# Decoder kernel: expert units in pairs, 512 columns per elementwise operation, new order tables

## What is computed

```python
probs = jax.nn.softmax(logits)
top_vals, top_idx = jax.lax.top_k(probs, K)             # K = 4, renormalised
comb = zeros((N, E)).at[arange(N)[:, None], top_idx].add(top_vals)
g = jnp.einsum('nh,ehi->eni', h, w_gate)                # E = 16, i = 176
u = jnp.einsum('nh,ehi->eni', h, w_up)
y = jnp.einsum('eni,eih->enh', silu(g) * u, w_down)
routed = jnp.einsum('enh,ne->nh', y, comb)
shared = silu(h @ sh_gate) * (h @ sh_up) @ sh_down      # 704 wide
out = routed + sigmoid(h @ sh_gate_w) * shared
```

## Time and profile before

| | us |
|---|---|
| median of 3 runs (lowest, highest) | 955.67 (949.19, 959.2) |
| the profiled execution, its whole time | 949.86 |
| its span from first to last instruction | 947.7 |
| PE busy | 828.1 (87%) |
| DVE busy | 631.5 (67%) |
| ACT, POOL busy | 369.4 (39%), 358.1 (38%) |

### The profile page before, as it was taken

One profiled execution on the slowest core, in us unless ns is written; L12 is line 12 of the kernel. 1 busy time (PEld: TensorE's weight loads), 2 busy tenths in 40 slices (PEclk: granted clock), 3 DMA queues, 4 the chain that ended last, 5 costly groups with the idle time before them and its releaser, 6 DMA issues.

```text
span 947.7 us, 12835 instructions
## 1 busy us (share of the span) xinstructions
PE 828.1 (87%) x4575; PEld 629.4 (66%) x4600; DVE 631.5 (67%) x1322; ACT 369.4 (39%) x796; POOL 358.1 (38%) x390
## 2 busy tenths in 40 slices
PE   6897656989999898889999997889999898679997
PEld 5675445753788786753788786753788786426886
DVE  5242699785456999884456999895456999764333
ACT  5121555327325444326324444327324444253110
POOL 4302396121034875220034976121034976000322
PEclk9998757999999999998999999999999999999999
DMA  7202400011026340311016340311024340300442
GB/s 224 102 12 82 154 36 0 1 56 60 1 63 226 118 131 0 112 67 50 1 55 232 117 129 6 111 48 68 1 57 150 117 134 0 111 2 1 145 155 78
DMA packets 26930, 76.13 MB, mean 80 GB/s; under 512 B 3436, under 2 KB 5420, under 8 KB 26228
## 3 DMA queue, kind: packets, MB, share of 16 engines
q1 hardware_dynamic: 26612, 75.26, 24.2%
q10 hardware_dynamic: 256, 0.07, 0.0%
HBM read 74.13 MB, written 1.11 MB: 79 GB/s over the span
## 4 chain that ended last, share of the span: by engine, by line
PE 53%; DVE 24%; issue 10%; POOL 7%; ACT 4%; DMA 1%; ACTq 0%; DVEq 0%; POOLq 0%; SPq 0%
PE B L806 26%; PE F L806 19%; DVE arena L1477 7%; POOL arena L493 3%; PE B L1107 3%; DVE arena L1489 3%; DVE nmx L1549 2%; PE F L835 1%; DVE q_t L1610 1%; ACT big L773 1%; DVE arena L1310 1%; POOL arena L567 1%; PE F L817 1%; DVE q_t L1615 1%; POOL rs L473 1%
## 5 line engine op out<-in xcount | busy, mean ns | idle before, releaser
L806 PE MATMUL B<-spare,mw 128*128 128x256 f32 x880 | 210.5, 383 | 6.3 <-DVE q_t L1615 5.1
L806 PEld LDWEIGHTS B<-spare,mw 128*128 128x128 f32 x880 | 164.6, 191 | 31.7 <-issue 8.5
L1477 DVE TENSOR_TENSOR_SCAN arena<-F,arena 128x512 f32<-128x512 f32 x128 | 148.8, 1206 | 1.6 <-ACT F L733 1.5
L584 POOL TENSOR_TENSOR spare<-q_t 128x256 f32<-128x256 f32 x112 | 80.7, 729 | 173.2 <-DVE q_t L1615 160.4
L493 POOL TENSOR_TENSOR arena<-du,arena 128x1024 f32<-128x1024 f32 x60 | 140.9, 2363 | 12.9 <-PE B L888 12.9
L733 ACT ACTIVATE F<-delta,a_neg 128x255 f32<-128x255 f32 x256 | 109.7, 467 | 58.2 <-DVE arena L1477 58.2
L806 PE MATMUL B<-mw,spare 128*128 128x256 f32 x448 | 117.6, 388 | 0.0
L795 ACT ACTIVATE q_t<-B 128x256 f32<-128x256 f32 x112 | 41.9, 380 | 149.9 <-PE B L806 149.8
L806 PEld LDWEIGHTS B<-mw,spare 128*128 128x128 f32 x448 | 86.5, 195 | 14.1 <-issue 1.6
L773 ACT ACTIVATE big<-B 128x512 f32<-128x512 f32 x128 | 69.4, 594 | 51.1 <-PE B L806 38.5
L1610 DVE SCALAR_TENSOR_TENSOR q_t<-q_t,B 128x256 f32<-128x256 f32 x112 | 46.6, 416 | 57.3 <-ACT q_t L795 57.0
(11 more groups left out here) (246 smaller groups left out, 1323.8 us busy)
## 6 DMA issues: line engine op xcount, KB each, us to landing
mw<-in_w_moe SPq DMA_DIRECT2D x112, 384.0 KB, 3.1
room<-in_w_f SPq DMA_DIRECT2D x4, 2544.0 KB, 9.2
arena<-b_out SPq DMA_DIRECT2D x32, 256.0 KB, 5.3
room<-in_w_l SPq DMA_DIRECT2D x4, 768.0 KB, 6.9
w_m<-in_w_m SPq DMA_DIRECT2D x1, 2112.0 KB
room<-in_w_l SPq DMA_DIRECT2D x4, 512.0 KB, 5.0
x_t<-in_x_t SPq DMA_DIRECT2D x4, 256.0 KB, 3.7
x_tok<-in_x_tok SPq DMA_DIRECT2D x4, 256.0 KB, 6.6
```

The source lines that it names most:

```text
L584: g.tensor_tensor(hid1[0:r, m % HID_RING, :], hraw[0:r, m % 3, :], crs[0:r, int(m >= MTE), :], ALU.mult)\
L806: return t_.matmul(dst, lhsT, rhs, start=start, stop=stop, skip_group_check=True)
L1477: v.tensor_tensor_scan(h, F[i][:, :], h, 0.0, ALU.mult, ALU.add)\
```

## The change

Two units 2p and 2p + 1 form a pair. `be{2p}` is now the gate half of pair p: PE puts both gates (4 calls) into one bank, K[0]; ACT takes one tanh of 512 columns; DVE makes `(tanh + 1) * gate` with 512 columns (`st{p}`). `be{2p+1}` is the up half: both ups (4 calls) into K[1], then the downs of pair p - 1 (4 calls); DVE multiplies by up with 512 columns (`gu{p}`), POOL multiplies by the routing row with 512 columns (`hid{p}`). Everything stays in one ring of three pairs (`PAIR_RING`), in place. PE waits at a gate half for `st{p-1}` and at an up half for `gu{p-1}`; in the last batch odd pairs use F[0], F[1] and the lag is two pairs. ACT waits for `hid{p-3}`. SP loads two units at the odd phases. The last pair keeps two 256-column products on DVE. Matmuls and bytes are the same.

```diff
...
+        thg = ao[:, 2:8, :].rearrange("p (r u) t -> p r (u t)", u=2)
...
+        def pair_banks(b, p):
+            return F[0:2] if b == B - 1 and p % 2 else K[0:2]
+        def pair_lag(b):
+            return 2 if b == B - 1 else 1
+        def pair_ring(p):
+            return thg[:, p % PAIR_RING, :]
...
+                if ph in BE and BE.index(ph) % 2 and BE.index(ph) >= 3:
+                    p = BE.index(ph) // 2
+                    for m in (2 * p - 2, 2 * p - 1):
+                        if m + MW_RING < MT1:
+                            sp.wait_ge(*pb.at(f"down{m}", b))
+                            sp.dma_start(mw[:, m % MW_RING, :], ins["w_moe"][m + MW_RING])\
+                                .then_inc(mw_in[m % MW_RING], 16)
...
+                if ph in BE and BE.index(ph) % 2:
+                    p = BE.index(ph) // 2
...
+                    pool.wait_ge(*db.at(f"gu{p}", b))
+                    if p >= HID_RING // 2:
+                        pool.wait_ge(*pb.at(f"down{2 * p + 1 - HID_RING}", b))
+                    s = 2 * p % HID_RING
+                    g.tensor_tensor(hid1[:, s:s + 2, :], pair_ring(p).rearrange("p (u t) -> p u t", u=2),
+                                    crs[:, int(2 * p >= MTE), :].unsqueeze(1).to_broadcast([P, 2, S]), ALU.mult)\
+                        .then_inc(gb.step(f"hid{p}"), 1)
...
+                if ph in BE and BE.index(ph) % 2 == 0:
+                    p = BE.index(ph) // 2
+                    act.wait_ge(*pb.at(f"g{p}", b))
+                    if p >= PAIR_RING:
+                        act.wait_ge(*gb.at(f"hid{p - PAIR_RING}", b))
+                    a.activation(pair_ring(p), pair_banks(b, p)[0][:, :], ACT.Tanh, scale=0.5)\
+                        .then_inc(ab.step(f"th{p}"), 1)
...
+                    p, u = divmod(BE.index(ph), 2)
+                    lag = pair_lag(b)
+                    if p >= lag:
+                        pe.wait_ge(*db.at(f"gu{p - lag}" if u else f"st{p - lag}", b))
+                    for j in range(2 if 2 * p + 1 < MT1 - 1 or u == 0 else 1):
+                        m = 2 * p + j
+                        slot = m % MW_RING
+                        if u == 0:
+                            pe.wait_ge(mw_in[slot], b * (len(range(slot, MT1, MW_RING)) * 16) + (m // MW_RING) * 16 + 16)
                         for k in range(KT):
                             c = u * D + k * P
+                            last = mm(pair_banks(b, p)[u][:, j * S:j * S + S], mw[:, slot, c:c + P], x5t[:, k, :],
                                       k == 0, k == KT - 1)
+                    last.then_inc(pb.step(f"u{p}" if u else f"g{p}"), 1)
+                    if u and p >= 1:
+                        expert_down(b, 2 * p - 2)
+                        expert_down(b, 2 * p - 1)
...
+                    p, u = divmod(BE.index(ph), 2)
+                    gates, ups = pair_banks(b, p)
+                    th = pair_ring(p)
+                    if u == 0:
+                        dve.wait_ge(*ab.at(f"th{p}", b))
+                        v.scalar_tensor_tensor(th, th, 1.0, gates[:, :], ALU.add, ALU.mult)\
+                            .then_inc(db.step(f"st{p}"), 1)
+                    else:
+                        dve.wait_ge(*pb.at(f"u{p}", b))
+                        dve.wait_ge(*db.at(f"st{p}", b))
+                        if 2 * p + 1 < MT1 - 1:
+                            v.tensor_tensor(th, th, ups[:, :], ALU.mult).then_inc(db.step(f"gu{p}"), 1)
...
```

More of the change, by code:

```diff
@@ L46 @@
 HID_RING = 4
+PAIR_RING = 3
 HALF = P // 2
@@ L341, in head @@
             return 8 * (q // 2) + 2 * j + q % 2
-        def gate_bank(b, m):
-            return K[m % (3 if b == B - 1 else 2)]
+        def pair_banks(b, p):
[4 more added lines that the diff above has]
+            return thg[:, p % PAIR_RING, :]
         def y_bank(dp):
@@ L788, in back @@
                     copy(crs.rearrange("p m n -> p (m n)"), K[3][:, :], ab, "crs", scale=0.5)
-                if ph in BE:
-                    m = BE.index(ph)
-                    act.wait_ge(*pb.at(f"gu{m}", b))
-                    if m >= 3:
-                        act.wait_ge(*db.at(f"gu{m - 3}", b))
-                    r = P if m < MT1 - 1 else HALF
-                    a.activation(thg[0:r, m % 3, :], gate_bank(b, m)[0:r, 0:S], ACT.Tanh, scale=0.5)\
-                        .then_inc(ab.step(f"th{m}"), 1)
+                if ph in BE and BE.index(ph) % 2 == 0:
[5 more added lines that the diff above has]
+                        .then_inc(ab.step(f"th{p}"), 1)
             run(front, back, af, ab, ORDER)
@@ L1208, in back @@
                 if ph in BE:
-                    m = BE.index(ph)
-                    slot = m % MW_RING
-                    pe.wait_ge(mw_in[slot], b * (len(range(slot, MT1, MW_RING)) * 16) + (m // MW_RING) * 16 + 16)
-                    r = 3 if b == B - 1 else 2
-                    if m >= r:
-                        pe.wait_ge(*db.at(f"gu{m - r}", b))
-                    for u in range(2 if m < MT1 - 1 else 1):
+                    p, u = divmod(BE.index(ph), 2)
[7 more added lines that the diff above has]
+                            pe.wait_ge(mw_in[slot], b * (len(range(slot, MT1, MW_RING)) * 16) + (m // MW_RING) * 16 + 16)
                         for k in range(KT):
                             c = u * D + k * P
-                            last = mm(gate_bank(b, m)[:, u * S:u * S + S], mw[:, slot, c:c + P], x5t[:, k, :],
+                            last = mm(pair_banks(b, p)[u][:, j * S:j * S + S], mw[:, slot, c:c + P], x5t[:, k, :],
                                       k == 0, k == KT - 1)
-                    last.then_inc(pb.step(f"gu{m}"), 1)
-                    if m >= 3:
-                        expert_down(b, m - 3)
+                    last.then_inc(pb.step(f"u{p}" if u else f"g{p}"), 1)
+                    if u and p >= 1:
+                        expert_down(b, 2 * p - 2)
+                        expert_down(b, 2 * p - 1)
                 if ph == "bout":
-                    for m in range(MT1 - 3, MT1):
+                    for m in range(MT1 - 2, MT1):
                         expert_down(b, m)
@@ L1605, in back @@
                 if ph in BE:
-                    m = BE.index(ph)
-                    dve.wait_ge(*ab.at(f"th{m}", b))
-                    r = P if m < MT1 - 1 else HALF
-                    up = gate_bank(b, m)[:, S:2 * S] if m < MT1 - 1 else gate_bank(b, m)[HALF:P, 0:S]
-                    v.scalar_tensor_tensor(thg[0:r, m % 3, :], thg[0:r, m % 3, :], 1.0, gate_bank(b, m)[0:r, 0:S], ALU.add,
-                                           ALU.mult).then_inc(db.step(), 1)
-                    if m >= 3:
-                        dve.wait_ge(*gb.at(f"hid{m - 3}", b))
-                    own(db, b)
-                    v.tensor_tensor(hraw[0:r, m % 3, :], thg[0:r, m % 3, :], up, ALU.mult)\
-                        .then_inc(db.step(f"gu{m}"), 1)
+                    p, u = divmod(BE.index(ph), 2)
[10 more added lines that the diff above has]
+                            v.tensor_tensor(th, th, ups[:, :], ALU.mult).then_inc(db.step(f"gu{p}"), 1)
+                        else:
+                            v.tensor_tensor(th[:, 0:S], th[:, 0:S], ups[:, 0:S], ALU.mult).then_inc(db.step(), 1)
+                            v.tensor_tensor(th[0:HALF, S:2 * S], th[0:HALF, S:2 * S], gates[HALF:P, S:2 * S], ALU.mult)\
+                                .then_inc(db.step(f"gu{p}"), 1)
                 if ph == "bout":
```

35 lines of the change are left out of this document (10 added, 25 removed), and 12 rows, old and new, of tables (AFTER_DVE, AFTER_PE).

## The result

The changed kernel takes 949.40 us (median of 20 runs, 947.07 to 950.81), the kernel before, run beside it, 955.94 (20 runs, 949.19 to 959.31 and two far above, 1020.13 and 1383.35, which the ratio leaves out). The ratio is 0.9944, 95% interval [0.9927, 0.9961]: 0.56% less, where 944 against 955.67 (-1.2%) was forecast. The profiled executions are 949.86 us before (span 947.7) and 950.81 after (span 949.0). So the two traces do not show the 6.5 us between the medians (5.6 without those two runs): they differ by +1.3 us of span. Before's trace comes from one of its shortest executions, after's from its longest.

The account below looks back on a forecast made before the run. PE bounds the kernel overall, DVE sets the scan's pace with PE close behind. Three merged stretches x (-2.8 - 0.3 - 1.2) = -12.9, +1.6 gives -11.3: 938.6, plus 5.8 carried over, 944 us; range 932 to 958.

Parts of the forecast that it names:

- Scan stage: First scan to output product in each merged stretch: 71.3 us against 74.1, so -2.8 us.
- The two waits that were followed: DVE in the scan stage: about 0.9 us for pair 7's tanh after s2, 0.4 for the ups of pair 6.
- Into the scan: Stretch ahead of the first scan, pair 4's gates moved behind d1: scan starts about 0.3 us earlier.
- +0.6 if the tanh is late: Bound ahead of the first scan: a late be8 tanh removes the cover, then +0.6 us.
- Head pairs to `ob`: Head stage of each merged stretch: DVE's waits go as maxima run beside the projection, -1.2 us, bounds -2.4 and +1.
- Attention of the back: Front scores to fa1 and behind, one more item ahead and one less after: 0, between -1.5 and +1.5 us.
- Last batch: PE-bound experts of the last batch: +0.5 us at the start, +1.1 at the end, together +1.6.
- The sum's frame: Whole-kernel total: the median's 5.8 us above before's profiled execution carried over, turning 938.6 into 944.4 us.
- the saving is eaten: Rival, chance 0.30: pairs' waits push PE back, scan keeps 1 us of gain, head stage gives nothing: 953 us.
- The slower rival: Rival, chance 0.12: PE waits for pairs at its banks in merged stretches, +4.2 us per stretch: 970 us.
- The rule of the Trainium skill: Cited with the slower rival (0.12): small idles between matmul groups cycling PSUM banks make PE's clock swing; about 1.6 us per stretch.

Follow-up runs that it names:

- second trace: The kernel before, unchanged, run and profiled once more: 953.94 us, ratio 1.0006, profiled span 952.5.
- last experiment: The kernel before with 2 throwaway matmuls ahead of each of the scores bm14 and bm15 in the merged stretches: 950.77 us, ratio 0.9981.
- ninth experiment: The changed kernel with filler at at0, before's attention positions and be8 behind d2, its 512-column pair operations cut into two of 256: 946.95 us.
- third experiment: The changed kernel with before's positions up to fg3 on PE, DVE and ACT, the new ones behind: 949.40 us, ratio 0.9973.
- fifth experiment: The changed kernel with five throwaway matmuls in PE's 2.50 us gap at at0: 948.13 us, ratio 0.9939.
- sixth experiment: The changed kernel with new positions up to the maxima behind oa, before's from there up to fg3: 949.52 us, ratio 0.9969.
- Three edits: On the changed kernel: be8 behind d2 (949.33 us), filler matmuls at at0 (948.13), before's attention positions behind oa (949.52); all together 939.95, ratio 0.9866.
- its twin: The changed kernel with at0 filler, before's attention positions and be8 behind d2, without extra last-batch filler: 939.95 us; with that extra filler 942.62.

## Why the prediction was right or wrong

**Scan stage, right in place, too large in the saving.** 71.3 us were forecast and 71.29, 71.30, 71.31 measured. DVE's prices were 682 and 685 (684 taken), POOL's 1,270 (1,350 taken; of the two bounds the lower, 1,278, was the right one: the broadcast routing row costs nothing), ACT's 591. The two waits that were followed are there, 0.9 for a tanh and 0.4 for ups, in the waits of the changed kernel inside the stage (columns as above):

```profile
DVE q_t L1624 <- ACT q_t L805: 1.2, 2, 0.9
DVE q_t L1630 <- PE B L816: 0.4, 1, 0.4
```

What was wrong is the base: 74.1 was the second stretch, the only one of the three with a low-clock piece early in its scan. Before's busy table there:

```profile
531.50:535.00 3.50, 3.50 (x11) 2.84 (x10) 3.40 (x4) 1.74 (x4) 3.50 (x3) 0.51 0.00 0
```

The stages beside it are 73.49 and 73.26. The saving was 2.3 on average, -7.0 in the trace where -8.4 stood. At full clock the stage of before is 73.24 (second trace) to 73.50 (last experiment), so the saving is 1.9 to 2.2 us, of which 1.1 is the width (ninth experiment) and the rest the pairing with its positions. The prices held: 73.24 less 0.4 of waits is 72.8 us of DVE's work, 71.30 less 1.6 is 69.7, and the prediction had 72.8 and 69.8. What was mis-sized are the waits of before: the 1.3 us that were left over in the stretch with the piece are 0.4 at full clock, so the new 1.6 took 1.2 us off the saving and not 0.2.

**Into the scan, right.** -0.2 for -0.3. The bound "+0.6 if the tanh is late" was not reached, but `be8` stood in the path: one phase later gives another 0.78.

**Head pairs to `ob`, the step that failed first.** The waits of DVE that were to go did go. The prediction named `bq3` behind the first head pair as a cost of copies (+1 at most). It costs through PE instead: the transposes had filled a gap, the gap of 2.50 us stayed empty, and PE ran its next eight records in 2.90 instead of 1.55 us. 29.51 became 31.0, so -1.2 became 0 by the mark. And the term was wrong even at full clock: the variance comes 1.5 us earlier, but the back's first exponential does not (30.29 us behind the head masks, 30.19 in before), so the gain returns as a longer next stage. The waits view of before could have told: PE's idle time at that place was 0.52 only because 1.95 us of `bq3` stood in front of it.

**Attention of the back, the other side of the same step.** Taken as 0 within 1.5, measured from the variance to the sum at full clock 37.96 against 36.04 in the last experiment, and 36.25 in the third with a low-clock piece: +1.7 to +1.9 per stretch, outside the bounds. The prediction looked only at what stands between `ob` and `fa1` and took the start as given. PE in order of time, after:

```profile
424.47 1.97 PE L816 MATMUL F<-room,arena 128*128 128x256 f32 x8
426.28 0.59 PE L816 MATMUL B<-q_t,k_t 128*128 128x512 bf16 x2
```

Before, the projection of `ob` came at 419.30 and lay hidden behind the maxima; now it is 5.2 us later, right ahead of DVE's mark, and the first exponentials' scores are queued behind it. ACT in order of time, before and after:

```profile
424.58 1.08 ACT L773 ACTIVATE big<-B 128x512 f32<-128x512 f32 x2 [6.55 <-PE B L806]
426.22 1.31 ACTq L764 DMA_DIRECT2D q_t<-nm_t  x2
427.58 1.09 ACT L773 ACTIVATE big<-B 128x512 f32<-128x512 f32 x2 [1.39 <-PE B L806]
```

```profile
426.69 1.08 ACT L784 ACTIVATE big<-B 128x512 f32<-128x512 f32 x2 [3.34 <-PE B L816]
428.05 1.29 ACTq L775 DMA_DIRECT2D q_t<-nm_t  x2
429.38 2.16 ACT L784 ACTIVATE big<-B 128x512 f32<-128x512 f32 x4 [1.36 <-PE B L1117]
```

Against the mark (425.36 before, 425.91 after) the first exponential starts 0.8 us ahead before and 0.8 us behind now: 1.6 us, which is the 1.5 that the variance comes earlier at full clock. From the head masks to the sum the changed kernel takes 67.47 us at full clock (fifth experiment), with before's front it is 67.34 at full clock and with the filler of the last experiment, and 67.22 at the least (third experiment, first stretch). So the two terms together were -1.2 per stretch in the forecast and are +0.1 to +0.2 at full clock; in the two traces they are +4.5 over three stretches, the rest of it with low-clock pieces. The sixth experiment has the same start and takes 0.65 off by the positions behind `oa`: 66.82, 0.4 less than before.

**Last batch, +3.6 for +1.6.** The chain that ended last still runs through PE's experts, but no longer in one piece of 70.3 us: its last piece of that length (start us, us, what), one of several that alternate between the banks K and F, is

```profile
928.33 6.91 PE B L816 x32
```

and behind it stands the wait of 1.1 us for the last wide product that was forecast (PE in order of time):

```profile
940.69 2.19 PE L816 MATMUL B<-mw,spare 128*128 128x256 f32 x8 [1.14 <-POOL spare L595]
```

At full clock the experts take 80.89, +1.9, 0.3 more than forecast. The other 1.7 is the low-clock piece at 866.6 (first table), where 16 records take

```profile
866.25 5.36 PE L816 MATMUL B<-spare,mw 128*128 128x256 f32 x16
```

**The sum's frame.** The forecast carried the 5.8 us between before's trace and its median over to the changed kernel. They are no constant: the second trace of before is 4.8 us longer, nearly all of it in three places with low-clock pieces. What the medians differ by, 6.5 us in the first session and 3.0 to 3.7 if the changed kernel's 949.40 is held against the 952.3 to 953.09 of before in the later ones, is therefore partly where such pieces fall. How much of it cannot be told from these runs: one trace of the changed kernel was taken.

**The rivals.** The outcome is nearest to "the saving is eaten" (the head stage gave nothing), but by another way: PE was not pushed back in the scan, and the scan kept its gain. The slower rival, waits at the pairs' banks, is refuted: PE waits 1.5 us there for DVE to have read a bank, DVE waits 1.6 us in the stage, and the clock is 1.00. The rule of the Trainium skill that was named with it (TensorE: Matmul & The Clock Gate, "A second HAM failure mode: psum-queue depth-cycling") is not borne out at the pairs' banks. The low-clock pieces came elsewhere, among others behind single idle gaps of 2.50 us at `at0` and of 0.57 and 0.69 us at the router. Behind the same two gaps at the router the third experiment ran at full clock (16 records in 3.70 us), so these gaps do not decide alone either.

## What to carry to other kernels

Before moving a piece of work off a slot, read what PE would do in that slot: a small block of matmuls ahead of a wait may earn its place only by keeping the clock at 2.4 GHz, and a few throwaway products in the gap then do the same. Take the base of a sum from a stage whose granted clock is 1.00, and compare stage by stage before comparing medians. Before a stage's gain goes into a sum, look whether the next stage waits for the mark at which it was read. An order change that shows in its stage and not in the median should be tried together with the others before it is dropped.

## What the runs showed of the hardware

Savings of a microsecond or two per stage did not show one by one. Three edits worth 2.7, 4.6 and 1.9 us by their own stages (`be8`, filler, attention) shortened the median by 0.1, 1.3 and -0.1 us singly, and by 9.4 together, when no low-clock piece was left in the merged stretches. Each single edit's trace has four or five such pieces between 182 us and the end of the last batch's first gates, as the changed kernel's has five, some at the same places and some at others.

The place of a low-clock piece is not set by the instructions ahead of it. The kernel before gave two different sets from the same code, the front of batch 0 ended at 181.50 in one trace and 184.61 in another with the same instructions, and a filler added at 850 us went with a low-clock piece at 633 us that its twin lacked. Why, no run here shows. The Trainium skill (TensorE: Matmul & The Clock Gate, "What's actually happening") says that the watch on PE's activity runs freely and that the same kernel therefore differs between runs; the two traces of before agree with it.

A low-clock piece costs 0 to 1.0 us in the scan stage, where DVE sets the pace, 1.5 to 1.6 behind the gap at `at0` (31.0 to 31.16 against 29.51), and 1.7 us in the last batch's experts, where PE sets it (82.58 against 80.89, and 80.64 against 78.96 in before).

Two 256-column operations of DVE that do not depend on each other take 0.75 us behind each other, one of 512 columns 0.69. From the first start to what follows, a tanh product and an up product took 2 x 0.86 = 1.72 for two single units (a chain, each operation reading the last), 1.52 for a pair in halves (537.41 to 538.93, ninth experiment) and 1.39 for a wide pair (542.26 to 543.65, changed kernel).
